# Turning the high part of a unit before the low part of the unit before it, in an attention kernel

## The chip, the cores and the metric

The kernel runs on one core of a Trainium2 chip. The metric is device time in microseconds (us), the median of several executions; less is better.

## The reference

Eight batches of 512 tokens of width 256 pass through gated cross-attention (16 heads of 64, 512 context rows of width 128), and then through a gated mixture of 8 experts, of which the router takes two:

```
x = x + tanh(g_xattn) * xattn(layernorm(x), ctx)
    xattn: scores = (q Wq)(ctx Wk)^T / 8;  attn = softmax(scores);  out = (attn (ctx Wv)) Wo + bo
x = x + tanh(g_ffn) * ffn(layernorm(x))
    ffn: sum over e of (x expert_w[e]^T + expert_b[e]) * comb[:, e]   (comb: top 2 of softmax(x gate_w^T))
```

## The kernel before

All products are made from numbers split into two f16 (or two fp32r) parts, a high part and a low part, so that three matmuls (high by high, high by low, low by high) stand for one in f32. The probabilities of the softmax are split in this way too, and they have to be turned (keys on the partitions) before they can be multiplied with the values.

The attention is cut into **units**: a unit is one pair of heads p (8 in a batch) by one tile t of 128 queries (4). A batch has 32 units, numbered u = 4p + t from 0 to 31 in this text, and the program has 256. A unit passes through the engines as follows.

- TensorE makes the scores into ST (L1443, 6 matmuls of 512 columns in all for the two heads).
- VectorE takes the maximum (L1001) and makes the shift (L1007).
- ScalarE makes the exponentials into pf (L822, two instructions), and copies them to f16 (L832). This copy is the **high part**; its semaphore is `p_hi`.
- GpSimd subtracts the high part from pf and writes the **low part** (L656); its semaphore is `p_lo`.
- SyncE's queue issues two DMAs that turn the parts from p_s into pt_s: L551 for the high part (it waits for `p_hi`, and for the slot of pt_s to be free), L558 for the low part (it waits for `p_lo`). Their landings are told by `hi_turned` and `lo_turned`.
- TensorE multiplies the turned parts with the values, 24 matmuls into PV (L1465, `values`). It waits for both `hi_turned` and `lo_turned` of the unit. VectorE then normalises.

There are 4 slots for the parts (p_s) and 8 for the turned parts (pt_s). ScalarE's copy of unit u waits for `hi_turned` of u - 4, GpSimd's low part for `lo_turned` of u - 4, and the exponentials for the low part of u - 3.

Each engine runs an order that is written out by hand: for each of the 32 rows of a batch a string names what stands there. Between the units there are all other jobs: projections (q, k, v), transposes of the activations, the output projection (wo), and the experts of the batch before (pair). The first batch and the last one have orders of their own, the six between them share one (LOOP). On TensorE the scores of unit u stand in row u. The values run some rows behind: the values of units 8 and 9 are in row 13, of 13 in row 17, of 17 in row 21, of 18 and 19 in row 23.

```
        "scores ot1 v2,1 logits values values k4", "scores",
```

is such a pair of rows (13 and 14 of LOOP). GpSimd's low part of unit 14 is held back in each LOOP batch (`hold1` to `hold3`), until VectorE has done the routing.

SyncE's queue issues all DMAs of the loop, in program order, and a wait in it holds up all that is behind it. Within a batch it takes: the load of the next batch's context (L567), then 32 times the turning of a unit; after unit 9 the load of the next batch's x (L582), 512 KB, which waits for GpSimd; after unit 31 the store of the output of the batch before (L592), which waits for the last jobs of the row.

Of the kernel before, what the change touches and what calls it, by code (L numbers as in the profile page):

```python
# [38 lines left out]
TT = TOKENS // P  # L39
# [19 lines left out]
PRO, FIRST, LOOP, LAST, EPI = "pro", "first", "loop", "last", "epi"  # L59
# [136 lines left out]
UNITS = PAIRS * TT  # L196
# [12 lines left out]
def summing(name):  # L209

    return name[0] in ("bias", "pair", "expert")
# [22 lines left out]
ON_PE = UNITS - 2  # L234
# [100 lines left out]
def build(nc, x, kv_t, g_xattn, g_ffn, wq, wk, wv, wo, bo, gate_t, expert_t, expert_b, out):  # L335
# [5 lines left out]
    with ctx:  # L341
# [144 lines left out]
        def unit_count(b, p, t):  # L486
            return b * (PAIRS * TT) + (p * TT + t + 1)
# [27 lines left out]
        def run(row, before=None, after=None):  # L515

            def turn(it):
                if before:
                    before(it)
                for n in range(UNITS):  # L520
                    row(it, n)
                if after:
                    after(it)
            turn(Iteration(FIRST, 0, 0))
            for b in range(1, BATCHES - 1):
                turn(Iteration(LOOP, b, b % LOOPED))
            turn(Iteration(LAST, BATCHES - 1, (BATCHES - 1) % LOOPED))

        @block.sync
        def _(sp):  # L530
            sp.dma_start(xin[:, 0:2, :], x_v[:, 0:2, :]).then_inc(x_half, 16)
            sp.dma_start(xin[:, 2:TT, :], x_v[:, 2:TT, :]).then_inc(x_in, 16)
            sp.dma_start(kvin[:, :], kv_v[:, 0, :]).then_inc(kv_in, 16)
            sp.dma_start(stage_q[:, :, early], wq_v[:, :, early]).then_inc(wq_in, 16)
            sp.dma_start(stage_q[:, :, rest], wq_v[:, :, rest]).then_inc(wq_rest_in, 16)
            sp.dma_start(stage_k, wk).then_inc(wk_in, 16)
            sp.dma_start(stage_v, wv).then_inc(wv_in, 16)
            sp.dma_start(gates[:, 0:1], g_xattn.partition_broadcast(P)).then_inc(small_in, 16)
            sp.dma_start(gates[:, 1:2], g_ffn.partition_broadcast(P)).then_inc(small_in, 16)
            sp.dma_start(bo_t[:, :], bo.partition_broadcast(P)).then_inc(small_in, 16)  # L540
            sp.wait_ge(const_pool, 1)
            for row0 in (0, 32, 64):
                sp.dma_start(eb[row0:row0 + EXPERTS, :], expert_b).then_inc(small_in, 16)
            sp.dma_start(gt_f[:, :, :], gate_t.rearrange("(c p) e -> p c e", p=P)).then_inc(small_in, 16)

            def turn_hi(it, p, t):

                n = unit_count(it.b, p, t)
                sp.wait_ge(p_hi, n)
                sp.wait_ge(pv_ready, n)  # L550
                sp.dma_start_transpose(pt_s[:, it.ring(p, t, PT_SLOTS), 0, :, :, :].rearrange("p h k q -> p (h k) q"),  # L551
                                       p_s[:, it.ring(p, t, P_SLOTS), 0, :, :].rearrange("p h k -> p (h k)"))\
                  .then_inc(hi_turned[t], 16)

            def turn_lo(it, p, t):

                sp.wait_ge(p_lo, unit_count(it.b, p, t) + PF_SLOTS)
                sp.dma_start_transpose(pt_s[:, it.ring(p, t, PT_SLOTS), 1, :, :, :].rearrange("p h k q -> p (h k) q"),  # L558
                                       p_s[:, it.ring(p, t, P_SLOTS), 1, :, :].rearrange("p h k -> p (h k)"))\
                  .then_inc(lo_turned[t], 16)  # L560

            def before(it):
                if it.kind != LAST:
                    sp.wait_ge(kmax_step, it.b + 1)
                    sp.wait_ge(kv_hi, it.b + 1)
                    sp.wait_ge(kv_lo, it.b + 1)
                    sp.dma_start(kvin[:, :], kv_v[:, bass.ds(it.b + 1, 1), :].rearrange("c a k -> c (a k)"))\  # L567
                      .then_inc(kv_in, 16)

            def row(it, n):  # L570
                if it.kind == FIRST and n == 0:
                    sp.dma_start(stage_o[:, :, :], wo.rearrange("(c p) n -> p c n", p=P)).then_inc(wo_in, 16)
                    sp.dma_start(stage_e[:, :, :], expert_t.rearrange("(c p) n -> p c n", p=P)).then_inc(ex_in, 16)
                if it.kind == FIRST and n == 1:
                    sp.wait_ge(w_lo, 2)
                if it.kind != LAST or n < ON_PE:
                    turn_hi(it, *divmod(n, TT))
                    turn_lo(it, *divmod(n, TT))
                if n == 9 and it.kind != LAST:
                    sp.wait_ge(ln1_done, it.b + 1)  # L580
                    sp.wait_ge(x_bias, it.b + 1)
                    sp.dma_start(xin[:, :, :], x_v[:, bass.ds(it.b * TT + TT, TT), :]).then_inc(x_in, 16)  # L582

            def after(it):
                if it.kind != FIRST:
                    store(it)

            def store(it):

                m = it.b - 1  # L590
                sp.wait_ge(job_free, it.done(JOBS, [name for name in JOBS[it.kind] if summing(name)][-1]) + BANKS)
                sp.dma_start(out_v[:, bass.ds(m * TT, TT), :], acc[:, :, :]).then_inc(y_out, 16)  # L592

            run(row, before=before, after=after)
            epi = Iteration(EPI, BATCHES, BATCHES % LOOPED)
            for t in range(TT):
                sp.wait_ge(job_free, epi.last_done(JOBS, ("bias", t // 2), ("expert", t, EC - 1)) + BANKS)
                sp.dma_start(out_v[:, (BATCHES - 1) * TT + t:(BATCHES - 1) * TT + t + 1, :],
                             acc[:, t:t + 1, :]).then_inc(y_out, 16)
            sp.wait_ge(y_out, 16 * BATCHES + 16 * TT)  # L600
# [982 lines left out]
```

## Time and profile before

| | |
|---|---|
| time, median of 3 runs | 953.1 us (952.51 to 953.34) |
| the profiled execution: its time | 954.97 us |
| its span, first to last instruction | 952.8 us |
| busy: TensorE | 918.6 us (96%) |
| busy: VectorE | 853.9 us (90%) |
| busy: ScalarE | 745.0 us (78%) |
| busy: GpSimd | 641.6 us (67%) |
| turning DMAs | 508, median 3.4 us from issue to landing |

The profile's page gives for each engine its busy time and its share of the span; the span is 2.2 us shorter than the execution's own time. The six LOOP batches make up the middle of the program. Times inside the program are counted from the span's first instruction. PE is TensorE, PEld its weight loads, DVE VectorE, ACT ScalarE, POOL GpSimd, and SPq SyncE's queue.

### The profile page before, as it was taken

To read this page: it belongs to the slowest core of one execution; us is meant where nothing else is said; L and a number is where in the kernel's file an instruction comes from. 1 tells how busy PE (TensorE), PEld (TensorE's weight loads), DVE (VectorE), ACT (ScalarE), POOL (GpSimd) and SP (SyncE) were. 2 spreads that over 40 slices of the span, in tenths; PEclk is the share of its full clock that TensorE was granted. 3 is DMA by queue.
4 is the path that set the end of the run, shared out by engine and by line. 5 is a ranking of instruction groups with operands and counts; after the bars stand their busy time and mean duration, and the time that the engine had idled before them with its cause. 6 is when DMAs were issued, how large, how long until landed. Compare 5 with 4: busy or idle time off the path is not lost.

```text
span 952.8 us, 28718 instructions
## 1 busy us (share of the span) xinstructions
PE 918.6 (96%) x11332; PEld 640.0 (67%) x11332; DVE 853.9 (90%) x1818; ACT 745.0 (78%) x1092; POOL 641.6 (67%) x439
## 2 busy tenths in 40 slices
PE   6788899999999999999999999999999999999997
PEld 4355556777667766777667776677667776667873
DVE  6899999998899989998999988998899988998758
ACT  3899899678995889768896789958898688978510
POOL 4667778586785868577685867858586776866400
PEclk9999999999999999999999999999999999999999
DMA  7599999899997989989999999989899799999800
GB/s 272 105 185 169 167 170 171 163 151 157 192 181 135 158 151 187 178 142 161 167 180 162 153 152 186 180 144 162 146 197 179 133 164 170 163 159 169 130 23 23
DMA packets 549141, 150.97 MB, mean 158 GB/s; under 512 B 537592, under 2 KB 547216, under 8 KB 548752
## 3 DMA queue, kind: packets, MB, share of 16 engines
q1 hardware_dynamic: 549008, 149.13, 92.8%
q8 instruction: 91, 1.49, 0.7%
q14 instruction: 42, 0.34, 0.1%
HBM read 11.70 MB, written 4.19 MB: 17 GB/s over the span
## 4 chain that ended last, share of the span: by engine, by line
PE 77%; DVE 15%; issue 3%; POOL 2%; ACT 1%; DMA 1%; SPq 0%; DVEq 0%; ACTq 0%; POOLq 0%
PE MB L1294 38%; PE PV L1465 16%; PE ST L1443 16%; PE MB L1306 4%; DVE nmax L1001 4%; DVE acc L942 2%; POOL p_s L656 1%; DVE ex_s L1169 1%; PE MB L1379 1%; DMA pt_s<-p_s 1%; PE MB L1384 1%; DVE o_n L1024 1%; DVE QL L981 1%; DVE v_s L992 1%; ACT pf L822 1%
## 5 line engine op out<-in xcount | busy, mean ns | idle before, releaser
L656 POOL TENSOR_TENSOR p_s<-pf,p_s 128x1024 f16<-128x1024 f32 x254 | 543.1, 2140 | 226.7 <-ACT p_s L832 178.5
L822 ACT ACTIVATE pf<-ST,shifts 128x512 f32<-128x512 f32 x512 | 324.0, 690 | 89.8 <-DVE shifts L1007 88.9
L1001 DVE TENSOR_REDUCE nmax<-ST 128x2 f32<-128x1024 f32 x256 | 310.6, 1217 | 15.9 <-PE ST L1443 14.8
L832 ACT ACTIVATE p_s<-pf 128x1024 f16<-128x1024 f32 x254 | 269.3, 1063 | 3.2
L1465 PEld LDWEIGHTS PV<-v_s,pt_s 128*128 128x128 f16 x6096 | 201.2, 97 | 43.1 <-issue 34.9
L1465 PE MATMUL PV<-v_s,pt_s 128*128 128x65 f16 x6096 | 215.5, 193 | 3.5 <-DVE o_n L1024 2.7
L1294 PE MATMUL MB<-ex_s,x2t_s 128*128 128x256 f16 (+1 forms) x1380 | 166.1, 275 | 0.1
L1294 PEld LDWEIGHTS MB<-ex_s,x2t_s 128*128 128x128 f16 x1380 | 131.9, 98 | 21.7 <-issue 1.3
L1443 PE MATMUL ST<-KH,QH 64*128 64x512 f16 x512 | 99.7, 386 | 8.7 <-ACT pf L822 6.9
L961 DVE SCALAR_TENSOR_TENSOR acc<-MB,m,acc 128x256 f32<-128x256 f32 x224 | 95.6, 476 | 4.4 <-PE MB L1294 3.6
L1294 PE MATMUL MB<-xt_s,wq_s 128*128 128x512 f16 x384 | 94.8, 383 | 3.3 <-DVE v_s L992 1.5
L1443 PE MATMUL ST<-KH,QL 64*128 64x512 f16 x512 | 97.9, 379 | 0.0
L1443 PE MATMUL ST<-KL,QH 64*128 64x512 f16 x512 | 97.6, 377 | 0.0
L1294 PE MATMUL MB<-wo_s,ot_s 128*128 128x256 f16 x744 | 91.1, 273 | 0.1
L1294 PEld LDWEIGHTS MB<-wo_s,ot_s 128*128 128x128 f16 x744 | 70.5, 98 | 16.2 <-issue 3.7
L1443 PEld LDWEIGHTS ST<-KH,QH 64*128 64x128 f16 x512 | 24.9, 93 | 63.8 <-issue 29.4
L1294 PEld LDWEIGHTS MB<-xt_s,wq_s 128*128 128x128 f16 x384 | 33.6, 98 | 44.5 <-issue 12.6
L1294 PE MATMUL MB<-wv_s,kv_s 128*128 128x512 f32 x192 | 60.6, 433 | 2.5 <-DVE QL L981 1.9
L1294 PE MATMUL MB<-kv_s,wk_s 128*128 128x512 f32 x192 | 61.8, 431 | 0.6 <-DVE xt_s L984 0.6
L1024 DVE TENSOR_TENSOR o_n<-PV,rden 128x256 f32<-128x256 f32 x127 | 53.9, 425 | 5.4 <-DVE rden L1021 1.2
L981 DVE SCALAR_TENSOR_TENSOR QL<-MB,q_out,QH 128x512 f16<-128x512 f32 x64 | 47.5, 743 | 12.0 <-ACT QH L739 12.0
L743 ACT ACTIVATE KH<-MB,k_mul 128x512 f16<-128x512 f32 x64 | 44.6, 697 | 15.3 <-PE MB L1294 11.8
(160 smaller groups left out, 1025.6 us busy)
## 6 DMA issues: line engine op xcount, KB each, us to landing
pt_s<-p_s SPq DMA_TRANSPOSE x508, 3.4
xin<-x SPq DMA_DIRECT2D x7, 512.0 KB, 4.3
out<-acc SPq DMA_DIRECT2D x7, 512.0 KB, 3.7
kvin<-kv_t SPq DMA_DIRECT2D x8, 256.0 KB, 4.5
stage_e<-expert_t SPq DMA_DIRECT2D x1, 2048.0 KB, 13.3
stage_o<-wo SPq DMA_DIRECT2D x1, 1024.0 KB, 8.8
stage_q<-wq SPq DMA_DIRECT2D x1, 768.0 KB, 6.6
xin<-x SPq DMA_DIRECT2D x2, 256.0 KB, 2.9
```

What stands on the lines that cost most here:

```text
L656: pool.tensor_tensor(p_s[:, slot, 1, :, :], pf[:, it.ring(p, u, PF_SLOTS), :, :], p_s[:, slot, 0, :, :], ALU.subtract).then_inc(p_lo, 1)
L743: last = act.activation(KH[:, it.pair_slot(name), :], m[:, :], ACT.Copy, scale=k_mul[:, of % 2:of % 2 + 1])
L822: last = act.activation(pf[:, (n - 1) % PF_SLOTS, i, :], ST[u % 2][:, i, :], ACT.Exp, bias=shifts[:, u % 2, i:i + 1])
L832: act.activation(p_s[:, it.ring(p, u, P_SLOTS), 0, :, :], pf[:, it.ring(p, u, PF_SLOTS), :, :], ACT.Copy).then_inc(p_hi, 1)
L961: last = dve.scalar_tensor_tensor(acc[:, t, :], m[:, DIM * i:DIM * (i + 1)], comb[:, t, e:e + 1], acc[:, t, :], ALU.mult, ALU.add)
L981: last = dve.scalar_tensor_tensor(l_s[:, slot_, :], m[:, :], scale, h_s[:, slot_, :], ALU.mult, ALU.subtract)
L1001: dve.tensor_reduce(nmax[:, t % 2, :, 0], ST[t % 2][:, :, :], AX.X, ALU.max, negate=True)\
L1024: dve.tensor_tensor(dst, outs[:, :, 0:HEAD], rden[:, :].unsqueeze(2).broadcast_to([P, TT, HEAD]), ALU.mult).then_inc(o_ready, 1)
L1294: last = pe.matmul(dst, s, m, start=(k == 0), stop=(k == n - 1))
L1306: last = pe.transpose(bank_[:, tile(t)], src(t), ident[:, :])
L1443: last = pe.matmul(ST[t % 2][:, i, :], queries[r, s, tile(t)], keys[r, s, :], start=(n == 0), stop=(n == len(terms) - 1))
L1465: last = pe.matmul(dst, pt_s[:, slot, a, i, k, :], v_s[:, c, k, (2 * p + i) % HEADS, :], start=(k == 0 and n == 0), stop=(k == TT - 1 and ...
```

## The change

Before, the queue takes for each unit its high part and then its low part. The change takes in row n the high part of unit n, and then the low part of unit n - 1. The last row of the batch (or of what the last batch turns by DMA, 30 units) takes its own low part as well. The two waits, their thresholds and all other engines stay as they were.

```
                 if it.kind == FIRST and n == 1:
                     sp.wait_ge(w_lo, 2)
-                if it.kind != LAST or n < ON_PE:
+                units = UNITS if it.kind != LAST else ON_PE
+                if n < units:
                     turn_hi(it, *divmod(n, TT))
-                    turn_lo(it, *divmod(n, TT))
+                    if n > 0:
+                        turn_lo(it, *divmod(n - 1, TT))
+                    if n == units - 1:
+                        turn_lo(it, *divmod(n, TT))
                 if n == 9 and it.kind != LAST:
                     sp.wait_ge(ln1_done, it.b + 1)
                     sp.wait_ge(x_bias, it.b + 1)
```

The first place is the end of one LOOP batch and the beginning of the next, on SyncE's queue. Before, with what each DMA waits for:

```order
L551 DMA_TRANSPOSE pt_s<-p_s 128x8x128 [waits pv_ready,p_hi]
L558 DMA_TRANSPOSE pt_s<-p_s 128x8x128 [waits p_lo]
L592 DMA out<-acc 128x4x256 [waits job_free]
L567 DMA kvin<-kv_t 128x512 [waits kv_lo,kv_hi,kmax_step]
L551 DMA_TRANSPOSE pt_s<-p_s 128x8x128 [waits pv_ready,p_hi]
L558 DMA_TRANSPOSE pt_s<-p_s 128x8x128 [waits p_lo]
```

The same place of the changed kernel, where "x2" is two such rows running (the store is line 596 there):

```order
L551 DMA_TRANSPOSE pt_s<-p_s 128x8x128 [waits pv_ready,p_hi]
L558 DMA_TRANSPOSE pt_s<-p_s 128x8x128 [waits p_lo] x2
L596 DMA out<-acc 128x4x256 [waits job_free]
L567 DMA kvin<-kv_t 128x512 [waits kv_lo,kv_hi,kmax_step]
L551 DMA_TRANSPOSE pt_s<-p_s 128x8x128 [waits pv_ready,p_hi] x2
L558 DMA_TRANSPOSE pt_s<-p_s 128x8x128 [waits p_lo]
```

The two low parts ahead of the store are those of units 30 and 31, and the two high parts behind the context load are those of units 0 and 1: from there on each low part stands one place further back than before, and each high part one place further forward, until the batch ends.

The second place is the load of x after unit 9, in the changed kernel (line 586 there):

```order
L551 DMA_TRANSPOSE pt_s<-p_s 128x8x128 [waits pv_ready,p_hi]
L558 DMA_TRANSPOSE pt_s<-p_s 128x8x128 [waits p_lo]
L586 DMA xin<-x 128x4x256 [waits x_bias,ln1_done]
L551 DMA_TRANSPOSE pt_s<-p_s 128x8x128 [waits pv_ready,p_hi]
L558 DMA_TRANSPOSE pt_s<-p_s 128x8x128 [waits p_lo]
```

The rows of before read alike, with the load at line 582, but stand for other units: ahead of the load there were the high and the low part of unit 9, and now the high part of 9 and the low part of 8. The low part of unit 9 has moved behind the load of x and behind the high part of unit 10.

## Rows read from the trace of the kernel before

**Rows 1.** The page: busy time of each engine, and the chain by engine.
```profile
PE 918.6 (96%) x11332; PEld 640.0 (67%) x11332; DVE 853.9 (90%) x1818; ACT 745.0 (78%) x1092; POOL 641.6 (67%) x439
PE 77%; DVE 15%; issue 3%; POOL 2%; ACT 1%; DMA 1%; SPq 0%; DVEq 0%; ACTq 0%; POOLq 0%
```

**Rows 2.** Stretches of one batch: us, busy of each engine, clock, DMA share, GB/s.
```profile
241.00:352.00 111.00, 111.00 (x1414) 78.66 (x1411) 101.42 (x221) 91.52 (x135) 79.95 (x54) 1.00 0.98 165
352.00:464.00 112.00, 111.31 (x1415) 78.81 (x1412) 101.81 (x221) 91.52 (x135) 80.04 (x54) 1.00 0.99 164
```

**Rows 3.** Waits: who for what, us, times, longest; last, GpSimd for L558's DMAs.
```profile
PEld PV L1465 <- DMA pt_s<-p_s: 1.9, 6, 0.4
PE PV L1465 <- DMA pt_s<-p_s: 0.2, 1, 0.2
PE PV L1465 <- issue: 0.5, 1, 0.5
...
  POOL p_s L656: 0.5, 1
```

**Rows 4.** SyncE's queue, timeline near units 17 to 20 of batch 2.
```profile
304.86 1.33 SPq L558 DMA_TRANSPOSE pt_s<-p_s  x1
307.68 1.23 SPq L551 DMA_TRANSPOSE pt_s<-p_s  x1
309.90 1.23 SPq L558 DMA_TRANSPOSE pt_s<-p_s  x1
311.22 2.32 SPq L551 DMA_TRANSPOSE pt_s<-p_s  x1
313.60 1.30 SPq L558 DMA_TRANSPOSE pt_s<-p_s  x1
314.99 1.28 SPq L551 DMA_TRANSPOSE pt_s<-p_s  x1
```

**Rows 5.** ScalarE's copies of units 18 and 20, and TensorE, same stretch.
```profile
306.59 1.06 ACT L832 ACTIVATE p_s<-pf 128x1024 f16<-128x1024 f32 x1
313.07 1.06 ACT L832 ACTIVATE p_s<-pf 128x1024 f16<-128x1024 f32 x1
...
308.48 0.39 PE L1443 MATMUL ST<-KH,QH 64*128 64x512 f16 x2
311.52 0.89 PE L1465 MATMUL PV<-v_s,pt_s 128*128 128x65 f16 x24
316.90 1.63 PE L1465 MATMUL PV<-v_s,pt_s 128*128 128x65 f16 x48
```

**Rows 6.** Landings of all turning DMAs of the low part, in us.
```profile
DMA to landing us min/median/max: 3.0/3.4/6.0
```

**Rows 7.** Batch 2: queue after unit 9; values 8, 9, 13; landings (276.05, 278.10).
```profile
275.59 0.37 SPq L582 DMA_DIRECT2D xin<-x  x1
276.05 1.24 SPq L551 DMA_TRANSPOSE pt_s<-p_s  x1
278.10 1.61 SPq L558 DMA_TRANSPOSE pt_s<-p_s  x1
279.80 1.26 SPq L551 DMA_TRANSPOSE pt_s<-p_s  x1
281.11 1.33 SPq L558 DMA_TRANSPOSE pt_s<-p_s  x1
282.53 2.52 SPq L551 DMA_TRANSPOSE pt_s<-p_s  x1
...
290.33 1.23 SPq L551 DMA_TRANSPOSE pt_s<-p_s  x1
295.74 1.23 SPq L558 DMA_TRANSPOSE pt_s<-p_s  x1
...
281.07 1.61 PE L1465 MATMUL PV<-v_s,pt_s 128*128 128x65 f16 x48
295.01 0.91 PE L1465 MATMUL PV<-v_s,pt_s 128*128 128x65 f16 x24
...
DMA to landing us min/median/max: 4.9/4.9/4.9
DMA to landing us min/median/max: 3.7/3.7/3.7
```

**Rows 8.** Batch 3: low part of 10, values of 8 and 9, and its landing.
```profile
391.22 2.19 SPq L558 DMA_TRANSPOSE pt_s<-p_s  x1
392.25 1.61 PE L1465 MATMUL PV<-v_s,pt_s 128*128 128x65 f16 x48
DMA to landing us min/median/max: 5.6/5.6/5.6
```

**Rows 9.** TensorE's longest wait before a lower clock; stretches after it.
```profile
PE PV L1472 <- DVE o_n L1024: 1.7, 1, 1.7
62.00:66.00 4.00, 2.95 (x15) 0.72 1.14 138
66.00:70.00 4.00, 3.92 (x61) 0.86 1.18 259
```

**Rows 10.** What SyncE's queue waited for, whole span.
```profile
SPq L558 <- POOL p_s L656: 139.8, 132, 4.2
SPq L551 <- ACT p_s L832: 101.5, 94, 18.7
```

## The prediction, made before the changed kernel was run

> **What bounds the kernel now.** I read the page first. TensorE is busy for 918.6 us of 952.8, and the chain that ended last is 77% TensorE [rows 1]. Next come the stretches of one batch each: in batch 2 TensorE is busy for 111.00 us of 111.00, at clock 1.00, with VectorE at 101.4, ScalarE at 91.5 and GpSimd at 80.0 [rows 2]. There is no idle time in which a later start of TensorE could be absorbed: whatever makes its `values` wait in batches 1 to 6 lengthens the program by the same amount. Then the waits: TensorE with its weight loads lost 2.1 us to the turning DMAs in the whole span, and 0.5 us more under "issue" at one `values` [rows 3]. So at most 2.6 us can be won by making the turned parts land sooner. Last I read SyncE's queue against TensorE's `values`, to see how long a turned part lies ready before it is used. This decides the case, because the change moves nothing else.
>
> The queue has idle time: it waited 139.8 us for low parts and 101.5 us for high parts [rows 10]. A turning DMA takes the queue 1.23 to 1.33 us when nothing disturbs it, and sometimes 1.6 to 2.5 [rows 4, 7]. It lands 3.0 to 6.0 us after its issue, median 3.4 [rows 6].
>
> **What the change does to a low part.** `values` of unit u needs both parts, and the low part is the later of the two both before and after. Before, it was issued as soon as GpSimd had made it and the queue was free. Now it also needs the high part of unit u + 1 to be issued first, so it waits for ScalarE's copy of the next unit. There are two regimes.
>
> Where the queue is behind (units 0 to 13, where DMAs follow each other with a gap of under 0.1 us, as 279.80 + 1.26 and then 281.11 [rows 7]), each low part is issued one place, some 1.35 us, later and each high part one place sooner. The number of DMAs and the rate of the queue are the same, so the backlog neither grows nor shrinks.
>
> Where the queue waits (from unit 14 on), the low part is late by the time from its being ready to the next copy, plus the 1.3 us of the high part's issue.
>
> Nobody gains from the earlier high part: only `values` and ScalarE's copy of u + 4 wait for it, and neither is held by it where it counts. GpSimd's low part of u + 4 waits for `lo_turned` of u, which comes later now. It waited for such a DMA once, 0.5 us [rows 3]; a delay of some tenths in more batches is covered by the exponentials, which need that low part only 3 units on. I cost it at nothing; uncovered it would be up to 1.35 us a batch, 8 us in all, which I leave to the top of the range.
>
> **The places where the room is gone.**
>
> Units 17 and 19. In batch 2, ScalarE's copy of unit 18 starts at 306.59 and ends at 307.65, and the high part goes out at 307.68. The low part of 17 went out at 304.86; now it goes at 307.68 + 1.29 + 0.05 = 309.02 and lands, with 3.3 us, at 312.3. `values` of 17 started at 311.52: **0.8 us late** [rows 4, 5]. The copy of unit 20 ends at 314.13, so its high part goes at 314.15, the low part of 19 at 315.5, and this lands at 318.8. `values` of 18 and 19 start at 316.90, the second of them at 316.90 + 0.74 = 317.64: 1.2 us late. The scores of unit 20 (308.48) stand ahead of `values` 17 on TensorE, so the copy of 20 is not pushed back by the first stall, and the two do not add: together they cost **1.25 us a batch**. The order of the rows is the same in the six LOOP batches, so 6 x 1.25 = 7.5 us. This term rests on the shortest landings and is the firm one.
>
> Unit 9. Its low part moves behind the load of x and the high part of unit 10. In batch 2 this is 276.05 + 1.24 + 0.05 = 277.34; it lands after 3.7 to 4.9 us, as its two neighbours there did, at 281.0 to 282.2, and `values` of 9 (the second of 281.07, so 281.81) waits 0 to 0.4 us [rows 7]. In batch 3 the place it takes is that of the low part of 10, issued at 391.22 and landed 5.6 us on at 396.8; `values` of 9 started at 392.25 + 0.74 = 392.99, so 3.8 us [rows 8]. The ends are 0 and 3.8 us a batch. Batch 3 is a bad one, in which TensorE is busy for 111.31 us of 112.00 [rows 2], so I take a value nearer to batch 2's: 0.7 x 6 = **4.2 us**.
>
> Long landings at units 13, 17 and 19. At 13 the high part of 14 goes at 290.33, so the low part of 13 at 291.62, landing at 295.0 in the short case, and `values` of 13 starts at 295.01 [rows 7]: no stall, but no room. From here each long landing costs its whole excess. Of the 13 turning issues of [rows 4, 7], three took 1.6 to 2.5 us, and beside such issues stand landings of 3.7, 4.9 and 5.6 us instead of 3.4 [rows 7, 8], 1.3 more in the mean. I estimate that one turning in four is hit, by 1.3 us. Of the three places, 17 and 19 count as one, for the reason above: 2 x 6 x 1/4 x 1.3 = **3.9 us**. The ends are 0 (never hit there) and about 8 (every second one).
>
> **Sum.** 7.5 + 4.2 + 3.9 = 15.6 us. The first batch and the last one have more room; I add nothing for them. What comes off: nothing at 14, where the queue stands 4.2 us for a held low part (291.56 to 295.74 [rows 7, 10]) and the high part of 15 now goes out meanwhile, since the low part of 15 still comes after it. On the profiled span, 952.8 + 15.6 = 968.4 us. This execution's own time was 954.97, 1.9 over the median of 953.1; as a difference the sum carries over: 953.1 + 15.6 = **968.7 us**.
>
> **Rivals.**
>
> *Nothing to be measured (953.1).* The stalls would have to vanish: ScalarE, freed of something, would make the copies of 18 and 20 more than 1 us sooner against TensorE. The copy of 20 follows its scores by 4.6 us (308.48 to 313.07), with maximum, shift and exponentials between, and the change frees none of these. For it: small delays may be recovered, as the queue has idle time. Against it: TensorE has none. Chance 0.07.
>
> *Faster (950.5).* The six waits of 1.9 us in all that the trace gives to turning DMAs are of the weight loads, and the first weights of a unit are of the high part. If it is the high part that lands last there, an earlier one removes them, and with the 0.2 and 0.5 of [rows 3] 2.6 us go: 953.1 - 2.6. It decides only if the low parts at 9, 13, 17 and 19 land within their room, which the times above deny by about 1 us. Chance 0.05.
>
> *Much slower, by the clock (979).* In the trace TensorE waited 1.7 us for VectorE in the first batch, and in the stretches about and behind it the granted clock was 0.72 and 0.86 [rows 9]; full speed is 2.4 GHz, the lower level 1.2. That cost 4 x 0.28 + 4 x 0.14 = 1.7 us beside the wait. If one stall in each LOOP batch grows to this size, 6 x 1.7 = 10 us come on top: 979. It decides from a single stall of about 1.7 us in a stretch where TensorE is otherwise less busy; my stalls are mostly 0.8 to 1.3, between stretches at 100% busy. Chance 0.08. The Trainium skill, "TensorE: Matmul & The Clock Gate", section "HAM oscillation — how this bites in real kernels", says that a TensorE which is made to wait for DMA between its bursts is put back to the half clock, and pays the fall and the rise each time; by that rule the loss would be the 10 us above. The trace agrees for that one place, and shows the clock at 1.00 in the batches as they are.
>
> *The forecast,* slower by the stalls alone: chance 0.80.
>
> **How the numbers follow.** The likeliest is 968.7. The low end is the firm term alone, 953.1 + 7.5 = 960.6; the high end adds to it 4.2 + 8 and some of a bad unit 9 or of the clock: 978. From 960 to 978 holds the forecast's cases and about half of the clock's. About 0.2% is what a measurement of this kernel can tell from no change (1.9 us): faster 0.05, within it 0.07, slower 0.88.
>
> **What would show it.** SyncE's queue: the low part's issue follows the high part of the next unit by 1.3 us nearly everywhere, and its wait for GpSimd falls from 139.8 us to a few tens, while the wait for ScalarE grows. TensorE: waits for turning DMAs at `values` of 9, 13, 17 and 19, some 15 us in place of 2.1. All busy times stay equal; LOOP batches last 113 to 115 us instead of 111.2, at clock 1.00. The prediction is wrong if `values` of 17 starts on time (then landing or copy is sooner than these rows say), if the stalls appear but batches stay at 111.2 us (then TensorE was not the bound), or if GpSimd waits for `lo_turned` and the exponentials slip with it.

## The result, and the profile after

The change makes the kernel **slower**: 979.9 us in the median of four executions (978.12 to 984.76), against 952.8 us for the kernel before on the same chip (951.96 to 953.34). The ratio is 1.029, with a 95% interval of 1.025 to 1.033. The forecast was 968.7 us with a range of 960 to 978, so the time lies 1.9 us above the range. The direction was right, and so was the mechanism in the six LOOP batches; but the loss is 27 us where I had worked out 15.6, and a part of it stands in the first batch, for which I had added nothing.

The page of the changed kernel (busy time of each engine, then the chain by engine), which answers to [rows 1]:

```profile
PE 924.8 (94%) x11332; PEld 642.1 (66%) x11332; DVE 857.5 (88%) x1818; ACT 745.6 (76%) x1092; POOL 641.1 (65%) x439
PE 44%; DVE 21%; issue 9%; POOL 9%; DMA 8%; ACT 8%; SPq 1%; DVEq 0%; POOLq 0%; ACTq 0%
```

The work is the same, instruction for instruction. What has changed is the chain: TensorE held 77% of it and now holds 44%, because the chain leaves TensorE at every `values` that had to wait for a turned part. The view of waits shows how much that was (who waited, for what: us, times, longest). The first line is of the whole span, the second of the LOOP batches alone (158 to 845 us), the last one GpSimd's waits for L558's DMAs:

```profile
PE PV L1469 <- DMA pt_s<-p_s: 18.0, 22, 2.0
...
PE PV L1469 <- DMA pt_s<-p_s: 16.9, 20, 2.0
...
  POOL p_s L660: 3.7, 3
```

Of the 0.2 us of [rows 3] there are 18.0 now. The stretch of batch 2, from its `values` of unit 2 to those of batch 3, answers to [rows 2] (length; busy and count of TensorE; clock; DMA share; GB/s):

```profile
274.30:387.70 113.40, 111.53 (x1415) 1.00 0.97 159
```

TensorE stands still for 1.87 us in it. The same stretch of the kernel before was about 111.2 us long, so 2.2 us were lost for waits of 1.9.

The loss can be watched where [rows 4] and [rows 5] stood. First SyncE's queue (start, us, operation), then ScalarE's copies of units 18 and 20, then TensorE's `values` of units 17, 18 and 19. In brackets stands the wait ahead of an instruction:

```profile
318.35 1.23 SPq L551 DMA_TRANSPOSE pt_s<-p_s  x1
319.63 1.33 SPq L558 DMA_TRANSPOSE pt_s<-p_s  x1
321.05 1.29 SPq L551 DMA_TRANSPOSE pt_s<-p_s  x1
322.39 1.31 SPq L558 DMA_TRANSPOSE pt_s<-p_s  x1
325.03 1.51 SPq L551 DMA_TRANSPOSE pt_s<-p_s  x1
326.59 1.30 SPq L558 DMA_TRANSPOSE pt_s<-p_s  x1
...
317.25 1.07 ACT L836 ACTIVATE p_s<-pf 128x1024 f16<-128x1024 f32 x1
323.95 1.06 ACT L836 ACTIVATE p_s<-pf 128x1024 f16<-128x1024 f32 x1
...
323.21 0.89 PE L1469 MATMUL PV<-v_s,pt_s 128*128 128x65 f16 x24 [0.65 <-DMA pt_s<-p_s]
328.48 0.90 PE L1469 MATMUL PV<-v_s,pt_s 128*128 128x65 f16 x24
330.01 0.89 PE L1469 MATMUL PV<-v_s,pt_s 128*128 128x65 f16 x24 [0.63 <-DMA pt_s<-p_s]
```

The copy of unit 18 ends at 318.32, its high part goes out at 318.35, and only then, at 319.63, the low part of unit 17. `values` of 17 would have started at 322.56 and starts at 323.21, some 3.6 us after that issue. The same happens around unit 19: copy of 20 until 325.01, high part 325.03, low part of 19 at 326.59, `values` at 330.01 instead of 329.38. So 0.65 + 0.63 = 1.3 us at this pair, where the prediction had 1.25.

Added up over the six LOOP batches, with the same view of TensorE, the waits before `values` are 9.4 us at units 17 and 19, 4.7 at unit 9, 1.6 at unit 13, and 1.3 at unit 11.

Last, what SyncE's queue waited for, beside [rows 10]:

```profile
SPq L551 <- ACT p_s L836: 191.9, 141, 18.8
SPq L558 <- POOL p_s L660: 121.3, 148, 2.1
```

### The profile page after: what moved, and what is told of

Read it like the earlier page. It is cut to its first block, busy times and chain, and to the rows that moved or that the text cites. A ratio compares the mean times of both kernels' runs of the same rounds, so it can differ in the third digit from the quotient of the medians.

```text
span 978.9 us, 28718 instructions
## 1 busy us (share of the span) xinstructions
PE 924.8 (94%) x11332; PEld 642.1 (66%) x11332; DVE 857.5 (88%) x1818; ACT 745.6 (76%) x1092; POOL 641.1 (65%) x439
## 4 chain that ended last, share of the span: by engine, by line
PE 44%; DVE 21%; issue 9%; POOL 9%; DMA 8%; ACT 8%; SPq 1%; DVEq 0%; POOLq 0%; ACTq 0%
PE MB L1298 22%; PE ST L1447 9%; PE PV L1469 9%; DMA pt_s<-p_s 8%; DVE nmax L1005 7%; POOL p_s L660 5%; ACT pf L826 4%; ACT p_s L836 3%; PE MB L1310 3%; DVE acc L946 2%; POOL xn L641 1%; DVE acc L965 1%; DVE o_n L1028 1%; POOL x L684 1%; DVE QL L985 1%
```

## The experiments

All kernels but x_in_hold put this into the kernel before, and differ in `CONDITION`, which says for which units m the low part goes out behind the next high part (`True` is the changed order; FIRST, LOOP and LAST are the kinds of batch). Two of them, x_one_row_on and ends_gate_parts_later, change one thing more, which is shown with them:

```
-                if it.kind != LAST or n < ON_PE:
-                    turn_hi(it, *divmod(n, TT))
-                    turn_lo(it, *divmod(n, TT))
+                units = UNITS if it.kind != LAST else ON_PE
+
+                def behind(m):
+                    return m < units - 1 and (CONDITION)
+                if n < units:
+                    turn_hi(it, *divmod(n, TT))
+                    if n > 0 and behind(n - 1):
+                        turn_lo(it, *divmod(n - 1, TT))
+                    if not behind(n):
+                        turn_lo(it, *divmod(n, TT))
```

### First set: the order again, its halves, and five units left out

`CONDITION` was `True` (all_again), `m < 14` (units_0_13), `m >= 14` (units_14_30), and `m not in (9, 11, 13, 17, 19)` (but_five).

> The changed order once more, as the yardstick of this set. Theory (room): the loss is the time by which low parts land after their values could start; near 980 us, with 16 to 20 us of waits of TensorE for turning DMAs at units 9, 11, 13, 17 and 19. Theory (clock): a part of the 27 us is TensorE at half clock after such a wait; then times of single runs scatter by several us with the number of falls, and this profile shows another number of falls than the first one did.

> Low parts stand behind the next unit's high part for units 0 to 13 only, where the queue is behind. Theory (room): TensorE waits at 9, 11 and 13 alone; in the changed kernel these took 4.7 + 1.3 + 1.6 = 7.6 us, so 960 to 961 us. Theory (queue): if the backlog itself grows and everything later inherits it, units 17 and 19 lose too and it is over 966. Theory (nothing in the backlog, one place is too little): 953.

> Low parts stand behind the next unit's high part for units 14 to 30 only. Theory (room): waits at 17 (6.2 us in the changed kernel) and 19 (3.1) and a little at 23 to 25, so 963 to 965 us; this and the run on units 0 to 13 add up to about the 27 us of the whole change, with what the clock adds. Theory (clock): if falls need several stalls close together, the two runs together lose clearly less than 27 us.

> The changed order, but the low parts of units 9, 11, 13, 17 and 19 go right behind their own high part, as before. Theory (room): only these five lack room, so the time returns to 953 to 956 us although 25 of 32 low parts of a batch are still late. Theory (queue or GpSimd): if late low parts hurt by what they hold up (slots of p_s, the exponentials), most of the loss stays, over 965 us.

Measured, on one chip on which the kernel before took 953.8 us:

| | median us (range, executions) | ratio (95%) |
|---|---|---|
| all_again | 979.8 (977.50 to 982.32, 4) | 1.029 (1.026 to 1.031) |
| units_0_13 | 962.5 (959.09 to 965.86, 4) | 1.010 (1.007 to 1.013) |
| units_14_30 | 968.9 (968.12 to 974.97, 4) | 1.018 (1.014 to 1.021) |
| but_five | 959.6 (957.42 to 962.89, 4) | 1.007 (1.004 to 1.009) |

The loss came back in full, and with it most of the pattern: of the 20 waits for turned parts in the LOOP batches after the change, 17 stand at the same unit of the same batch in all_again too (unit 9 of batch 3 waited 1.88 us and then 2.05). Their lengths are less steady: unit 17 of batch 5 waited 2.03 us and then 0.62, and the sum was 15.0 us in place of 16.9. The halves cost 8.7 and 15.0 us, 23.7 together against 26.0 for the whole; both lie above what I had expected of them (960 to 961 us, and 963 to 965). The second one also delays unit 25 of the first batch, where its profile shows 2.1 us of its loss. TensorE's waits for turned parts in the LOOP batches, in units_0_13 and then in units_14_30 (0.9 of the 9.2 us stand at unit 11 of batch 3, whose own order is the one of before):

```profile
PE PV L1472 <- DMA pt_s<-p_s: 5.4, 8, 1.5
...
PE PV L1472 <- DMA pt_s<-p_s: 9.2, 11, 1.8
```

In but_five there is none left in the LOOP batches, only three short ones under "issue", all at unit 12, and batch 1 is as long as it was before, though 26 low parts of it still go out late:

```profile
157.90:269.00 111.10, 111.10 (x1415) 78.89 (x1414) 101.51 (x221) 91.61 (x135) 80.07 (x54) 1.00 0.95 163
...
PE PV L1472 <- issue: 1.7, 3, 0.7
```

So nearly all of the loss of the LOOP batches sits at the five named units: together they last 667.6 us here, against 665.8 before and 686.8 after the change. What stays, 1.8 us, is about what the three waits at unit 12 and one of 0.9 us at unit 0 of the last batch add up to, less the 0.7 that TensorE waited before. But the kernel stays 5.7 us slower, and its stretch from `values` 2 of the first batch to those of batch 1 lasts 107.5 us instead of 103.2. That was the part for which I had added nothing.

### Second set: units 17 and 19, and the two ends

`CONDITION` was `it.kind == LOOP and m == 17` (only_17), `it.kind == LOOP and m == 19` (only_19), `it.kind == LOOP and m in (17, 19)` (both_17_19) and `it.kind != LOOP` (ends_only).

> Only the low part of unit 17 in the six LOOP batches stands behind the next high part. Theory (room): 0.8 to 1.0 us a batch from the landing alone, with long landings 6 us in all: 958 to 960 us, waits at 17 alone. If a single late low part is absorbed somewhere, 953 to 955.

> Only the low part of unit 19 in the LOOP batches. Theory (room): 1.2 us a batch with the shortest landing, 7 to 9 us in all, so 960 to 962 us, waits at 19 alone and longer than those of 19 in the whole change.

> The low parts of 17 and 19 in the LOOP batches. Theory (they share one loss): the copy of unit 20 is made from scores that stand ahead of the values of 17, so the stall at 17 does not push it back, and the two cost together hardly more than 19 alone: 961 to 963 us. Rival (they add): the sum of the two single runs, 965 us or more.

> The changed order in the first and the last batch alone, the LOOP batches as before. The prediction had nothing for these. If the rest of the loss of the run without the five units (5.7 us) sits there, this one takes 957 to 960 us, with waits at units 25 and 31 of the first batch and 0 and 7 of the last; if it sits in the LOOP batches after all, 953.

Measured, beside 953.6 us for the kernel before:

| | median us (range, executions) | ratio (95%) |
|---|---|---|
| only_17 | 961.7 (960.51 to 962.90, 4) | 1.009 (1.006 to 1.012) |
| only_19 | 964.4 (962.43 to 966.18, 4) | 1.011 (1.008 to 1.014) |
| both_17_19 | 967.3 (963.12 to 968.69, 4) | 1.013 (1.010 to 1.017) |
| ends_only | 959.1 (957.78 to 960.72, 5) | 1.005 (1.003 to 1.007) |

TensorE's waits for turned parts in the LOOP batches, of only_17, only_19 and both_17_19 in turn:

```profile
PE PV L1472 <- DMA pt_s<-p_s: 5.8, 6, 1.7
...
PE PV L1472 <- DMA pt_s<-p_s: 8.5, 6, 2.2
...
PE PV L1472 <- DMA pt_s<-p_s: 8.4, 10, 1.5
```

A single late low part per batch costs TensorE 5.8 or 8.5 us, and the two together 8.4, not 14.3. In these profiles the two places share one loss, as the prediction had it: a wait at 17 takes most of the wait at 19 with it. In batch 2, for one, the waits of both_17_19 are 0.71 and 0.34 us, and only_19 waits 1.02 there. The times do not decide it: +8.1, +10.8, and +13.7 for both lies midway between one shared loss (10.8) and the sum (18.9), and 967.3 us is in the range that I had given to the rival, 965 or more. The profiled execution of both_17_19 took 963.12 us, the shortest of the four, at a granted clock of 0.992; the other three took 967.2 us and more at 0.986 to 0.987, and what they lost beyond it stands in no trace.

ends_only changes nothing in six of eight batches and costs 5.5 us. Its LOOP batches are no longer than before: five of 111.14 to 111.19 us and the sixth, the shorter one before too, of 108.8. What happens in its first batch, on TensorE, VectorE and GpSimd, and then two stretches (TensorE, its weight loads, VectorE, ScalarE, GpSimd; clock; DMA share; GB/s):

```profile
120.27 0.88 PE L1472 MATMUL PV<-v_s,pt_s 128*128 128x65 f16 x24 [0.94 <-DMA pt_s<-p_s]
129.06 2.72 PE L1301 MATMUL MB<-wo_s,ot_s 128*128 128x256 f16 x12 [2.80 <-DVE KL L988]
...
124.49 2.45 DVE L1138 SCALAR_TENSOR_TENSOR eb_s<-eb,eb_mul,eb_s 8x256 fp32r<-8x256 f32 x1
128.18 0.74 DVE L988 SCALAR_TENSOR_TENSOR KL<-MB,k_mul,KH 128x512 f16<-128x512 f32 x1
...
124.54 2.13 POOL L663 TENSOR_TENSOR p_s<-pf,p_s 128x1024 f16<-128x1024 f32 x1 [1.30 <-ACT p_s L839]
...
125.00:128.90 3.90, 1.27 (x12) 0.88 (x10) 3.87 (x5) 1.73 (x4) 1.67 (x1) 1.00 0.70 135
128.90:133.00 4.10, 3.94 (x22) 2.21 (x24) 2.97 (x7) 3.27 (x5) 2.85 (x2) 0.59 0.43 84
```

In the kernel before, VectorE's same small instruction falls between two subtractions of GpSimd (one ends at 122.64, the next starts at 123.67):

```profile
122.80 0.47 DVE L1131 SCALAR_TENSOR_TENSOR eb_s<-eb,eb_mul,eb_s 8x256 fp32r<-8x256 f32 x1
```

Read it as a chain. The low part of unit 25 is late, and its `values` wait 0.94 us. VectorE comes to `eb_s` at 124.49, within 0.05 us of GpSimd's start on a low part, and the instruction takes 2.45 us instead of 0.47, until 126.94, which is 0.27 after GpSimd's end at 126.67. With it KL comes late, TensorE waits 2.80 us for that, and behind this wait the granted clock of the next 4.1 us is 0.59 on average, a mixture of its two levels (1.2 and 2.4 GHz). A wait of 0.94 us has grown to some 4.3: the first batch, counted as above, lasts 107.6 us. The profile of the changed kernel has like figures (a wait of 0.77 at unit 25, `eb_s` 2.45 us, 2.6 us of wait for KL, clock 0.57 in the four microseconds behind), and so have but_five and x_one_row_on (waits of 0.75 and 1.22, `eb_s` 2.45 us in both, waits for KL of 2.6 and 2.8).

The Trainium skill, "SBUF — State Buffer", section "Who interferes with whom", says that VectorE and GpSimd share one pair of ports as an exclusive lock, that a VectorE instruction with two inputs in SBUF falls under it when GpSimd's reads SBUF, and that whichever is second is blocked completely until the first is done. The trace agrees for this pair of instructions: 0.47 us apart from GpSimd's, 2.45 us beside it.

### Third set: the units with room, and two attempts at the load of x

loop_roomy has `it.kind == LOOP and m not in (9, 11, 13, 17, 19)`. x_one_row_on has the changed order everywhere and the load of x one row later:

```
-                if n == 9 and it.kind != LAST:
+                if n == 10 and it.kind != LAST:
```

x_in_hold keeps the order of before, and in LOOP batches issues the load of x and the high part of 15 ahead of the low part of 14, for which the queue waits:

```
+                held = 14 if it.kind == LOOP else None
...
-                    turn_hi(it, *divmod(n, TT))
+                    if n != 15 or it.kind != LOOP:
+                        turn_hi(it, *divmod(n, TT))
+                    if n == held:
+                        load_x(it)
+                        turn_hi(it, *divmod(n + 1, TT))
                     turn_lo(it, *divmod(n, TT))
-                if n == 9 and it.kind != LAST:
+                if n == 9 and it.kind == FIRST:
+                    load_x(it)
```

> LOOP batches in the changed order but for units 9, 11, 13, 17 and 19; first and last batch as before. Theory (room): 27 low parts a batch are late and none of them is waited for, so 953 us, no change that can be measured, LOOP batches of 111.2 us. Theory (GpSimd or queue): a few us over it.

> The changed order with the load of x one row later, so that the low part of 9 goes ahead of it. Theory (the load is what hurts unit 9, by its own issue and by the transfers that land long beside it): the waits at 9, 4.7 us in the changed kernel, go to under 1 us, those at 10 to 12 grow by some of it, and it takes 975 to 979 us. If the one place further back is all that matters, nothing changes: 980.

> The order of before, but in the LOOP batches the load of x and the high part of 15 go out while the queue would stand still for the held low part of 14. It takes the load out of the stretch in which the queue is behind. Expected: the waits of TensorE in batch 3 (0.7 us and some tenths in batch 4) go, 951 to 953 us, hardly to be told from no change; slower if the statistics of x, which need the load, come late (the load would land at about 297, they start at 300 in batch 2).

Measured, beside 953.2 us for the kernel before:

| | median us (range, executions) | ratio (95%) |
|---|---|---|
| loop_roomy | 957.4 (954.63 to 960.45, 10) | 1.005 (1.003 to 1.006) |
| x_one_row_on | 977.1 (975.39 to 982.01, 4) | 1.025 (1.022 to 1.028) |
| x_in_hold | 954.2 (951.08 to 955.24, 12) | 1.0005 (0.9994 to 1.0015) |

**loop_roomy** was to cost nothing and cost 4.2 us. In its profiled execution TensorE waits once for a turned part, before `values` of unit 12 in batch 6. The trace puts that under "issue":

```profile
PE PV L1472 <- issue: 1.1, 1, 1.1
```

The low part of unit 12 landed 4.4 us after its issue there; at the same place of the kernel before it had landed 2.4 us ahead of its `values`. GpSimd's waits for `lo_turned` add a little: before the low part of unit 7 of batch 6 it waits 1.3 us, with that its job behind (xn) comes late, and TensorE waits for it:

```profile
718.73 0.66 PE L1313 MATMUL MB<-ident,xn 128*128 128x128 f32 x4 [0.23 <-POOL xn L644]
```

The LOOP batches together are 1.0 us longer in this execution than before (666.8 us against 665.8). So "the other units have room" holds nearly, not fully: unit 12 has none when a landing is long. The whole span is 2.2 us longer (955.0 against 952.8), and 1.5 of that lie ahead of `values` 2 of the first batch, where the two kernels run the same order at a different granted clock (before, then loop_roomy):

```profile
0.00:49.70 49.70, 35.61 (x218) 0.93 0.73 186
0.00:51.20 51.20, 37.59 (x218) 0.87 0.68 185
```

So the profile accounts for its own 2.2 us, of which 1.0 can be laid to the late low parts. It leaves open why the median of ten executions is 4.2 us higher.

**x_one_row_on** takes away the wait at unit 9, and the wait at 11 grows from 1.3 us in all to 5.8. The waits in the LOOP batches fall only from 16.9 to 13.5 (the view has 14.2, with 0.6 at unit 0 of the last batch):

```profile
PE PV L1472 <- DMA pt_s<-p_s: 14.2, 17, 1.9
```

So in the stretch where the queue is behind, the load is one more slot, which delays whichever low part stands behind it. And unit 11 had the least room of all to begin with: in the trace of the kernel before, its low part landed 0.3, 1.6, 0.1, 0.1, 1.1 and 0.7 us ahead of its `values` in the six LOOP batches, that of unit 9 1.9 to 4.8 us and that of unit 13 1.5 to 4.0. In the changed kernel the waits at 9 push the `values` of 11 back, and so hide much of what 11 lacks.

**x_in_hold** takes away all of TensorE's waits in the LOOP batches; its batch 2 is full, and the queue takes the load and a high part at 292.97 and 293.60, while it stands waiting in the kernel before [rows 7]:

```profile
265.50:376.70 111.20, 111.20 (x1417) 78.88 (x1416) 101.61 (x221) 91.64 (x135) 80.02 (x54) 1.00 1.01 162
...
291.65 1.23 SPq L551 DMA_TRANSPOSE pt_s<-p_s  x1
292.97 0.53 SPq L590 DMA_DIRECT2D xin<-x  x1
293.60 2.40 SPq L551 DMA_TRANSPOSE pt_s<-p_s  x1
297.06 3.31 SPq L558 DMA_TRANSPOSE pt_s<-p_s  x2
```

Batch 2 of before was as full, and in the whole of the LOOP batches there was little to win: 664.8 us here against 665.8, about what batches 3 and 4 had lost before. The medians show no difference. I found no version that beats the kernel before.

### Fourth set: what the first batch does with one late low part

`CONDITION` was `it.kind == FIRST and m == 25` (first_25_only) and `it.kind != LOOP and not (it.kind == FIRST and m == 25)` (ends_but_25). ends_gate_parts_later is ends_only with the job that makes `eb_s` moved down by one row of VectorE's order of the first batch:

```
-        "maximum normalise take shift ll", "maximum take take shift", "maximum normalise take gp shift",
-        "maximum take shift ll take take take",
+        "maximum normalise take shift ll", "maximum take take shift", "maximum normalise take shift",
+        "maximum take shift ll take take take gp",
```

> One single low part of the program stands behind the next unit's high part: that of unit 25 in the first batch. Theory (chain): its stall of about 0.9 us pushes VectorE's eb_s into GpSimd's subtraction; in executions in which VectorE comes second there the clock falls too, and it costs 2 to 5 us: 954 to 958 us. Rival (plain stall): 0.9 us, 953.5 to 954.5.

> The changed order in the first and the last batch, without unit 25 of the first. Theory (chain): first batch back to 103.2 us, eb_s at 0.47 us; the last batch keeps its waits at 7, 23 and 24 of some 1.3 us: 954 to 955.5 us. If it stays at 958 or more, the first batch loses elsewhere.

> The changed order in the first and the last batch, with VectorE's two small instructions that split the gate weights and the expert bias (eb_s) moved from row 30 to the end of row 31. Theory (chain): eb_s no longer stands ahead of KL, so even if it takes 2.45 us there, TensorE's wait for KL of 2.8 us goes below 1 us and no fall of the clock follows at 129 us; the wait at 25 stays: 954.5 to 957 us, 2 to 3 us under the run of both ends. Rival (the long instruction only fills time in which VectorE would wait anyway): no change, 959.

Measured, beside 953.2 us for the kernel before:

| | median us (range, executions) | ratio (95%) |
|---|---|---|
| first_25_only | 956.3 (952.68 to 960.18, 12) | 1.004 (1.003 to 1.006) |
| ends_but_25 | 955.5 (952.95 to 957.25, 12) | 1.003 (1.002 to 1.004) |
| ends_gate_parts_later | 960.0 (957.80 to 960.99, 6) | 1.007 (1.006 to 1.009) |

ends_but_25 did what was expected: in its profile the first batch is back at 103.3 us and `eb_s` at 0.47. Of the 2.3 us that it still costs its profile shows 1.1, behind `values` 2 of the last batch. In first_25_only, one late low part in the whole program costs 3.1 us in the median, and its twelve times lie in two groups: six from 952.68 to 955.15, and six from 957.46 to 960.18. The profiled execution is of the first group. There VectorE is 0.12 us ahead of GpSimd (first VectorE, then GpSimd):

```profile
124.46 0.47 DVE L1138 SCALAR_TENSOR_TENSOR eb_s<-eb,eb_mul,eb_s 8x256 fp32r<-8x256 f32 x1
...
124.58 2.34 POOL L663 TENSOR_TENSOR p_s<-pf,p_s 128x1024 f16<-128x1024 f32 x1 [1.03 <-ACT p_s L839]
```

`eb_s` takes 0.47 us, GpSimd 2.34 instead of 2.13, and no lower clock follows. That the upper group is the executions in which GpSimd is first is an inference: none of them was profiled, though the four profiles with `eb_s` at 2.45 us at this place (after the change, ends_only, but_five, x_one_row_on) lose 4.2 to 4.5 us in their first batch. Two profiles with the same late unit and `eb_s` at 0.47, all_again and units_14_30, lose 2.2 and 2.1, although TensorE waited longer at unit 25 there (1.39 and 1.24 us, against 0.75 to 1.22 in the four). So the long instruction, with the wait and the lower clock behind it, is worth a good 2 us in these six.

Moving the job did not help. It met GpSimd again at its new place, and the wait went from KL to the scores that need ScalarE's pf (VectorE's row, then TensorE's waits from 104 to 140 us):

```profile
129.59 2.47 DVE L1138 SCALAR_TENSOR_TENSOR eb_s<-eb,eb_mul,eb_s 8x256 fp32r<-8x256 f32 x1
...
PE ST L1450 <- ACT pf L829: 3.3, 3, 2.4
```

The expectation that the loss would go was wrong. What it was to show, that the long instruction and not the late part itself is the larger cost, is not shown by this run: the long instruction came back at another place, together with the loss and with a lower clock (from 136.6 us on).

## Why the prediction was right, and where it was wrong

**The step that failed** is the term for the two ends, put at nothing because they "have more room", without a row of them having been read. ends_only puts it at 5.5 us, and the first batch of the changed kernel is 4.2 us longer in the profile. The term of the LOOP batches had its cause right and its size too low: 15.6 us worked out, 21.0 lost. Either miss alone would have left the time inside the range (974 us both times); together they took it out.

**TensorE bounds the kernel, and any wait at `values` lengthens it.** Right. The LOOP batches, counted from `values` 2 of batch 1 to those of batch 7, last 686.8 us after the change and 665.8 before, and with the five units put back 667.6, three of them at 111.1 to 111.2 us as before.

**Where the room is gone.** Right for 17, 19, 9 and 13. The terms against the waits of the profile: 17 and 19 had 7.5 and half of the 3.9 for long landings, 9.5 us, measured 9.4. Unit 9 had 4.2, measured 4.7. Unit 13 had the other half of the 3.9, measured 1.6. All together 15.6 us worked out and 16.9 measured, with unit 11. That 4.2 and 4.7 agree so well is in part luck: 0.7 us a batch was my choice between 0 and 3.8, and batch 3, for which I had worked out 3.8, waited 1.88. **That 17 and 19 share one loss** is what the waits show (5.8, 8.5, and 8.4 for both), while the times leave it open.

**Units 11 and 12** were not in the sum. Unit 11 waits 1.3 us, and 5.8 when the load stands ahead of it. I had read, in the stretch where the queue is behind, only the low part whose slot the load takes, and worked out the room of 9 and 13 alone, though unit 11 had less than either. Nor is the delay there one slot of 1.35 us each time: counted from `values` 2 of the batch, the low parts of units 3 to 8 went out 0.4 to 2.8 us later than before in batches 1 to 5, and that of unit 9 1.6 to 4.1 us later.

**"The first batch and the last one have more room; I add nothing for them."** Wrong, and the largest error: the two ends alone cost 5.5 us. The rows that I read were all of LOOP batches. The first batch has an order of its own, and unit 25 stands there as 17 and 19 do in the LOOP batches: before, its low part landed 3.1 us ahead of its `values`, but behind the copy and the high part of unit 26 it goes out 3.6 us later, counted from `values` 2. The wait of 0.8 to 0.9 us moves VectorE onto GpSimd. first_25_only puts this one low part at 3.1 us of the 5.5. Without unit 25 the ends still cost 2.3 us; the last batch's waits at `values` in the profile after the change are 0.8, 0.3 and 0.6 us, of which the first is at its unit 0 (the view lays it to VectorE) and the last stands under "issue".

**The sum took each wait at its own length.** Too small. In batch 2 2.2 us were lost for 1.9 of waits, about 0.1 more for each of its waits. In the LOOP batches, counted up to `values` 2 of the last one, 21.0 us were lost for 16.9: 0.8 is the wait at unit 0 of the last batch, 1.7 one lower clock in batch 6, and the 1.6 that remain are what follows each wait, less what batches 3 and 4 had lost before. The lower clock follows the longest wait but one (`values` of 8 and 9, then two stretches with TensorE's busy time and the clock):

```profile
747.63 0.89 PE L1469 MATMUL PV<-v_s,pt_s 128*128 128x65 f16 x24
750.47 0.88 PE L1469 MATMUL PV<-v_s,pt_s 128*128 128x65 f16 x24 [1.95 <-DMA pt_s<-p_s]
...
744.00:751.20 7.20, 5.25 (x74) 1.00 1.08 207
751.20:754.70 3.50, 3.50 (x19) 0.51 1.14 161
```

**The rival of the clock** gave 979 us, and the time is 979.9. Yet its mechanism is only a small part of the loss. It asked for a lower clock in each LOOP batch; there was one in six, and one in the first batch. It would be wrong to take the agreement of the numbers for agreement of the causes. What it said of the condition holds in part: TensorE had worked 5.25 us of the 7.20 before, and waited 1.95; but the waits of 2.03 us at unit 17 of batch 5 and of 1.88 at unit 9 of batch 3 were followed by clock 1.00. The other profiles say the same. In all_again the clock fell behind a wait of 1.97 us and not behind one of 2.05, in only_19 behind 2.19 and not behind 2.08. The length of the wait alone does not decide. The fall in all_again, on TensorE:

```profile
778.00:783.00 5.00, 4.88 (x43) 0.66 0.88 172
```

The Trainium skill, "TensorE: Matmul & The Clock Gate", section "HAM oscillation — how this bites in real kernels", has TensorE fall back each time that it is starved by a DMA between bursts, in an example whose waits for DMA last about 3 to 5 us, longer than any here. In the trace of the changed kernel a fall came behind one of the three waits of about 2 us, and behind none of the shorter ones of the LOOP batches. The wait that the prediction set beside this rule, 1.7 us in the first batch, was for VectorE and not for a DMA.

**GpSimd's waits for `lo_turned` cost nothing.** Nearly right. It waited 3.7 us in all, three times, instead of 0.5. Two of the waits, of about 1 us, are at unit 7 of batches 3 and 6. They do not make a low part late that counts: GpSimd had finished that of unit 9 of batch 3 at 397.68 us, and the queue took it at 401.84. What they do reach is GpSimd's job xn, for which TensorE needs it soon after: the way to `values` of unit 6 is 0.2 us longer in batch 3 and 0.1 in batch 6. The third wait, of 1.7 us, is at unit 29 of the last batch, whose low part then still stood 3.1 us ready before the queue took it.

**The queue's wait for GpSimd "falls from 139.8 us to a few tens"** was wrong: it fell to 121.3. Its wait for ScalarE grew as said, from 101.5 to 191.9. The queue waits at L551 for the next copy first, and then in many rows still for the low part behind it.

**The account of the difference,** between the two profiled spans (978.9 and 952.8): 26.1 us, of which 21.0 lie in the LOOP batches, 4.2 in the first batch, 1.5 ahead of `values` 2 of the first batch, and -0.5 behind those of the last. The LOOP part is 16.9 of waits, 0.8 of the wait at unit 0 of the last batch, 1.7 of one lower clock, and 1.6 of the rest. The 1.5 ahead are not the change's doing: loop_roomy and x_in_hold, which leave the first batch as it was, reach the same point at 51.2 us too. At the end, the kernel before had a lower clock of its own (0.62 from 920.0 to 924.5 us), which the changed kernel had not. The medians differ by 27.1.

**What stays open.** Why the medians of some kernels lie above what their profiles show in the LOOP batches: 4.2 us against 1.0 in loop_roomy, 8.1 against 5.1 in only_17, 13.7 against 8.7 in both_17_19. It is a share of the loss that no wait explains, and it may well be in the changed kernel too. Why some landings are long: of the 39 low parts that took over 4.4 us after the change, 31 did so in all_again too, which points to what else runs there, but to what was not tried. And whether the long `eb_s` is all of the difference between the two groups of first_25_only.

## What to carry to other kernels

In a queue that takes its waits in program order, a transfer moved behind another inherits the other's wait: compare, for every place and not for the middle of the program alone, the new landing with the moment of use. A full slot of room is not always enough: unit 12 of batch 6 had 2.4 us, nearly two slots, and still waited 1.1 us in loop_roomy. Where one engine is busy all the time, such a delay of under 1 us is lost in full, with 0.1 to 0.2 us on top. And a short delay can make the instructions of two engines meet, as `eb_s` and GpSimd's low part did here: look at what starts within 0.1 us of what before trusting a sum of waits.

## What the runs showed of the hardware

**A collision decided by less than 0.1 us.** VectorE's instruction on 8x256 numbers took 2.45 us in ends_only, where the records have it start 0.05 us ahead of GpSimd's 128x1024 subtraction. In all_again they have the same 0.05 us, and in units_14_30 too, and there the other engine was held up (all_again, VectorE, then GpSimd):

```profile
126.52 0.47 DVE L1138 SCALAR_TENSOR_TENSOR eb_s<-eb,eb_mul,eb_s 8x256 fp32r<-8x256 f32 x1
...
126.57 2.41 POOL L663 TENSOR_TENSOR p_s<-pf,p_s 128x1024 f16<-128x1024 f32 x1 [1.74 <-ACT p_s L839]
```

The recorded starts don't tell the winner at this distance; the durations do. Here it costs GpSimd 0.3 us, and there VectorE 2 us.

**The granted clock moves the time of one kernel.** In the kernel before, executions with a mean granted clock of 0.995 took 950.6 to 951.9 us, and those with 0.988 took 954.3 to 955.2. After the change, 0.992 went with 978.12 us and 0.983 with 984.76. So it helps to compare executions at an equal clock where 2 us matter: the one at 0.992 is about 25 us above those of the kernel before at 0.992 (952.6 to 953.2 us, and the profiled one 955.0). It does not settle everything: two executions of all_again, both at 0.987, took 977.50 and 981.87 us. A part of the difference arises at the very start: the profiled executions reach `values` 2 of the first batch between 48.7 us (only_19, clock 0.96 up to there) and 51.9 (all_again and only_17).
